# TensorE issues heads 0 to 2's scores one step earlier, ahead of two transposes, with waits per head

## The reference

```
bias = (adj + adj)[:, None]
a = q @ k.T * D**-0.5 + bias            # 16 heads of 32 columns, 512 x 512 each
a = where(any(a != 0, -1), a, -inf)
p = softmax(a); p = where(isnan(p), 0, p)
o = p @ v                               # heads put side by side
x = layernorm(x + o @ Wo.T)
```

## Time and profile before

| what | value |
|---|---|
| time, median of 3 runs | 2225.41 us (2225.25 to 2225.51) |
| the profiled execution's own time | 2224.26 us |
| its span | 2222.5 us |
| granted TensorE clock, mean | 0.989 |
| TensorE busy | 2125.2 us, 96% |
| VectorE busy | 1580.2 us, 71% |
| ScalarE busy | 1570.8 us, 71% |
| GpSimd busy | 301.8 us, 14% |
| chain that ended last, TensorE's share | 71% |

### The profile page before, as it was taken

One profiled execution on the slowest core, in us unless ns is written; L12 is line 12 of the kernel. 1 busy time (PEld: TensorE's weight loads), 2 busy tenths in 40 slices (PEclk: granted clock), 3 DMA queues, 4 the chain that ended last, 5 costly groups with the idle time before them and its releaser, 6 DMA issues.

```text
span 2222.5 us, 42446 instructions
## 1 busy us (share of the span) xinstructions
PE 2125.2 (96%) x14627; PEld 1683.8 (76%) x14627; DVE 1580.2 (71%) x4012; ACT 1570.8 (71%) x3509; POOL 301.8 (14%) x659
## 2 busy tenths in 40 slices
PE   6999999589999999999999999999999999999996
PEld 5778887467777777777777777777777777777774
DVE  5887877366767676767676768686868686868675
ACT  3544443187878787878787878787878787878785
POOL 0000000110202020202020202020202020202011
PEclk9999999799999999999999999999999999999999
DMA  6444342677777777777777777777778777777761
GB/s 237 160 155 148 133 150 94 130 119 127 141 129 139 128 140 128 140 126 142 134 133 133 134 133 135 132 136 132 134 130 138 134 135 131 136 135 133 131 100 45
DMA packets 149008, 297.18 MB, mean 134 GB/s; under 512 B 14514, under 2 KB 14546, under 8 KB 148690
## 3 DMA queue, kind: packets, MB, share of 16 engines
q1 hardware_dynamic: 137490, 256.97, 61.8%
q0 software_dynamic: 11328, 37.76, 6.0%
HBM read 110.12 MB, written 50.33 MB: 72 GB/s over the span
## 4 chain that ended last, share of the span: by engine, by line
PE 71%; issue 13%; ACT 8%; DVE 6%; DMA 1%; POOL 0%; SPq 0%; DVEq 0%; ACTq 0%; POOLq 0%
PE bank L605 28%; PE bank L651 17%; PE bank L635 11%; PE bank L620 8%; ACT prob L872 3%; DVE prob L1166 2%; PE bank L525 2%; ACT probT L770 2%; PE bank L542 2%; PE bank L577 1%; PE bank L643 1%; DVE z L1130 1%; DVE st_ln L1123 1%; DMA qp<-stage_q 1%; ACT v L844 1%
## 5 line engine op out<-in xcount | busy, mean ns | idle before, releaser
L1166 DVE CUSTOM_DVE_ANT_0 prob<-bank,adj_sb 128x512 f32<-128x512 f32 x1024 | 657.7, 686 | 140.8 <-PE bank L620 140.8
L872 ACT ACTIVATE prob<-prob,neg_max 128x512 f32<-128x512 f32 x1024 | 731.3, 723 | 9.4 <-DVE neg_max L1175 5.4
L770 ACT ACTIVATE probT<-bank 128x512 f32<-128x512 f32 x832 | 460.3, 594 | 320.4 <-PE bank L651 318.0
L651 PEld LDWEIGHTS bank<-ident,prob 128*128 128x128 f32 x4096 | 463.6, 140 | 111.9 <-issue 51.9
L651 PE MATMUL bank<-ident,prob 128*128 128x128 f32 x4096 | 541.1, 275 | 5.6 <-ACT probT L770 4.3
L620 PE MATMUL bank<-kp,qp 128*128 128x512 f32 x1024 | 348.5, 422 | 31.1 <-DVE row_max L1166 21.6
L1180 DVE COPY probT<-bank 128x512 f32<-128x512 f32 x192 | 131.6, 686 | 235.9 <-PE bank L651 235.9
L635 PE MATMUL bank<-probT,v 128*32 128x256 f32 x4096 | 247.6, 382 | 0.8 <-issue 0.8
L620 PEld LDWEIGHTS bank<-kp,qp 128*128 128x128 f32 x1024 | 176.4, 190 | 64.5 <-DVE row_max L1166 34.4
L872 ACT ACTIVATION_READ_ACCUMULATOR prob<-prob,neg_max 128x1 f32 x1024 | 204.4, 200 | 0.0
L605 PE MATMUL bank<-xT,wkT 128*128 128x512 f32 x768 | 202.3, 399 | 0.0
(11 more groups left out here) (112 smaller groups left out, 2088.7 us busy)
## 6 DMA issues: line engine op xcount, KB each, us to landing
kp<-stage_k SPq DMA_DIRECT2D x256, 256.0 KB, 6.7
qp<-stage_q SPq DMA_DIRECT2D x256, 256.0 KB, 8.5
x_raw<-in_x_dram SPq DMA_DIRECT2D x16, 1024.0 KB, 7.5
adj_raw<-in_adj_t_dram SPq DMA_DIRECT2D x16, 1024.0 KB, 9.7
outT_spill<-outT SPq DMA_DIRECT2D x16, 1024.0 KB, 5.1
v<-outT_spill SPq DMA_DIRECT2D x16, 1024.0 KB, 15.1
z<-in_x_dram POOLq DMA_DIRECT2D x64, 256.0 KB, 3.1
adj_sb<-in_adj_dram SPq DMA_DIRECT2D x64, 256.0 KB, 8.1
```

Source lines behind the costliest of these rows:

```text
L651: ins = nc.tensor.transpose(t_bank[j % 2][:, mt * P:(mt + 1) * P], prob[:, s % 2, j, mt * P:(mt + 1) * P], ident[:, :])
L770: return nc.scalar.activation(dst, src, ACT.Copy, scale=scale)
L872: nc.scalar.activation(prob[:, s % 2, j, :], prob[:, s % 2, j, :], ACT.Exp, scale=2.0, bias=neg_max[:, s % 2, j:j + 1], accum_out=row_sum[ ...
L1166: nc.vector.tensor_tensor_reduce(prob[:, s % 2, j, :], s_bank[j][:, :], adj_sb[:, t, :], 1.0, LOWEST, ALU.add, ALU.max, row_max[:, g % 2, ...
```

## The change

In the diff, `scores` is called with step s+2 for heads 0 to 2, after the second dense half and ahead of the transposes of heads 2 and 3; it is called with step s+1 for head 3 as before. The prologue issues one such set more. The scores of heads 0 to 2 now wait each for its own bank: head 0 for all four maxima of the step before the one that it belongs to (bank 0 was last read by head 3), head 1 for the second and head 2 for the third maximum. On VectorE each head waits for the transposes of the same head of the step two before.

```diff
-                if heads[0] == 0:
-                    need(pe, s_max, 64 * b + J * s)
-                else:
-                    pe.wait_ge(s_max, 64 * b + J * s + 1)
                 for j in heads:
+                    if j == 3:
+                        pe.wait_ge(s_max, 64 * b + J * s + 1)
+                    else:
+                        need(pe, s_max, 64 * b + (J * s if j == 0 else J * (s - 1) + j + 1))
                     mm(s_bank[j][:, :], qp[:, g % 2, j, t * P:(t + 1) * P], kp[:, g % 2, j, :],
                        start=True, stop=True).then_inc(s_ps, 1)
...
             scores(0, 0, (3,))
+            scores(0, 1, (0, 1, 2))
...
-                    def next_scores(heads):
-                        if s + 1 < STEPS:
-                            scores(b, s + 1, heads)
+                    def next_scores(heads, ahead):
+                        if s + ahead < STEPS:
+                            scores(b, s + ahead, heads)
                         elif not last:
-                            scores(b + 1, 0, heads)
+                            scores(b + 1, s + ahead - STEPS, heads)
...
-                    next_scores((0, 1, 2))
...
-                    next_scores((3,))
+                    next_scores((3,), 1)
...
+                    next_scores((0, 1, 2), 2)
                     pe.wait_ge(pT_act, copies_act(b, s, 1))
                     prob_transpose(b, s, 2)
...
                 if heads[0] == 0:
                     dve.wait_ge(adj1_in[t], 16 * b + 16)
-                    need(dve, p_ps, 64 * b + J * (s - 1))
                     if t == 0:
                         need(dve, live_chain, 3 * (G * b + g - 1))
                 for j in heads:
+                    need(dve, p_ps, 64 * b + J * (s - 2) + j + 1)
                     wait_apart(dve, s_ps, 64 * b + J * s + j + 1)
```

## The result

The changed kernel takes 2270.78 us (median of 5 runs, 2268.62 to 2272.95) against 2225.51 us; the ratio is 1.0205, 95% interval [1.0192, 1.0218]. The profiled execution took 2268.62 us with a span of 2266.8 us, 44.3 us over the span before. The granted clock is 1.00 in the batches of both kernels, so it has no part in this. The forecast was 2259 us in a range of 2240 to 2277. A batch lasts 113.57 us from its last transposes to the next batch's, mean of 14, against 110.86.

The account below looks back on a forecast made before the run. TensorE, busy 109.35 of 110.8 us a batch, was taken as the bound. Terms 1.56 + 0 + 0.60 + 0.25 - 0.65 + 0.13 = 1.89 a batch, x14 = 26.5, with the ends 33.9 us: 2259.3, range 2240 to 2277.

Parts of the forecast that it names:

- Part 1: Steps 1, 3, 11, 13, 14, 15: head 3's score waits 0.16 us, loses 0.10 overlap; 1.56 per batch.
- E+1.39: Start of head 3's score, 1.39 us after the recorded end of the transposes closing a step; 1.90 before the change.
- Part 2: Heads 0 to 2's scores, made two steps ahead, wait for head 3's maximum: 0.16 us to spare, cost 0.
- Part 3: Transposes of heads 2 and 3 come 0.70 us later; through ScalarE's ReLU, Y in step 5 comes 0.60 later.
- Part 4: Step 4's spread of reciprocals: its chain comes 0.45 us later with 0.2 spare; cost 0.25.
- Part 5: Gains: step 8's wait at head 3's score shrinks 0.30 us, step 9's transpose waits filled, 0.35; sum -0.65.
- Part 6: Step 14: next batch's head 0 scores wait for the fourth packed-q transfer; +0.13 us, bounds 0 and 0.7.
- The ends: Outside the middle batches: batch 0 costs about 3.4 us, the last batch 4.0.
- Rival (c): Slower: head 3's maximum late in odd steps or q's last pair 0.7 later; 0.7 to 1.0 a batch, 2272; chance 0.2.
- (a): Faster: early scores keep VectorE fed, step 8's wait at head 3's score goes whole; 2202 us, chance 0.06.
- (b): No change: needs bias-to-score hand-over of 0.58, not 0.74; gains and Y's delay cancel; 2226 us, chance 0.06.
- S3(9): Head 3's score for step 9, issued in step 8: still late by about 0.9 us, waiting for VectorE.

Follow-up runs that it names:

- the first run: Changed kernel, per-head waits kept, with heads 0 to 2's scores back in their old place; 2225.0 us, ratio 1.0002.
- the run with step 6 alone: Kernel before, with the per-head waits and only step 8's scores made early, in step 6; 2220.78 us, ratio 0.9983.
- the run with three waits taken away: Kernel before with per-head waits, step 8's scores early, its bias ahead of copy, ReLUs one step earlier, step 9's heads 0 and 1 copied before x; 2221.28 us.

## Why the prediction was right, and where not

- Part 1, S3 behind the copy: right to 0.04, place and price. Steps 1, 3, 11 and 13 grew by 0.27 to 0.30 for 0.26. Step 15 grew by 0.22 because it also lost the 0.08 that it used to wait for q. E+1.39 came as written. It is shown by the bias ahead of the copy.
- Part 2, no wait at S012 for head 3's maximum: right; the odd steps show S3's 0.27 and little else (0.03 or 0.04 in steps 3, 11 and 15 is not explained). No price of the per-head waits: shown by the first run, in the old place.
- Part 3, Y in step 5: 0.59 for 0.60, shown by step 4 in the old place.
- Part 4, the spread in step 4: 0.23 for 0.25. It went with the bias ahead of the copy.
- Part 5, step 8: -0.40 for -0.30, the mechanism (ScalarE's copy limits it) seen in the run with step 6 alone. Step 9 failed: -0.02 for -0.35. I let S012(11) fill the wait at T2, and forgot that S012(10) had left the same stretch: T2 waits for a copy that hangs on step 8's last dense matmul, from which it stands 3.46 us away in both kernels. The matmuls between are as many as before. In step 9 of batch 5 of the changed kernel, with step 8's last dense matmul at 1073.94:

```profile
1074.38 0.60 ACT L771 ACTIVATE v<-bank 128x512 f32<-128x512 f32 x1 [1.39 <-PE bank L605]
...
1076.76 1.07 ACT L771 ACTIVATE probT<-bank 128x512 f32<-128x512 f32 x2
...
1077.40 0.90 PEld L651 LDWEIGHTS bank<-ident,prob 128*128 128x128 f32 x8 [0.82 <-ACT probT L771]
```

ScalarE waits for the dense work, copies v, and then goes on without a gap, through two exponentials and the copy of x, to the copy that T2 waits for. From its copy of v to T2 it is 3.03 in each of batches 1 to 14 of both kernels. The wait at T2 did not fill, it grew: from 0.32 on the weight load to 0.82. No run moves step 9's scores alone. But the run with three waits taken away bears out that ScalarE's order sets this wait: with heads 0 and 1 copied ahead of x, step 9 fell by 0.28.

- Part 6, q: the mechanism was right and the size wrong: 0.13 forecast, 0.54 measured (0.89 in step 14 less S3's 0.27, and less the 0.08 that step 15 no longer waits). I wrote that the last pair "queue behind the first pair, which I take to hide it". It does, but the queue itself had moved, from k's packing on: q landed 0.41 later, which is the whole of what was missing. The bound of 0.7 held it. The 2 us of fixed cost in the Trainium skill (DMA: Bandwidth & Descriptors, Latency and other measured facts) is no guide under such a queue: the last transfer of the next batch's q took 7.2 to 9.8 us from issue to landing in all of these kernels (batches 2 to 13).
- The ends: up to the end of batch 0 it cost 3.5 for 3.4, the last batch 2.9 for 4.0. The first agreement is in part luck: 0.7 of the 3.5 comes before step 1 of batch 0, and the end of batch 0 lies at 551.2 us in the kernel before and at 552.8 in the one with the old place and the new waits, for no reason that the change gives.
- Together: (2.71 - 1.89) x 14 = 11.5 us more, 1.1 less at the end, which is the 10 us between forecast and span. Rival (c) had q's delay as one of its two ways, at 0.7 to 1.0 a batch; it came at half of that. Rivals (a) and (b) are out: no step but 8 gained clearly, and the hand-over from bias to S3 stayed at 0.74, where (b) needed 0.58.
- Of the signs, TensorE's wait in more places, Y and S3(9) (0.89 late by its weight load) came as written, and so did VectorE's wait ahead of its copy. One did not: VectorE's idle time before scores was to nearly vanish, and 95.0 of 140.8 us are left.
- The range held, but with the two misses on the same side: step 9 and q together are 0.74 a batch, 10 us.

The Trainium skill (PSUM — Partial Sum Buffer, Engine vs sequencer instructions) says that matmuls start in program order, while a weight load may overlap matmuls in flight. The trace agrees: S3 of step 8 starts at 1066.20, and the 32 matmuls of weigh_v behind it start 0.43 later, though the last copy that they read had ended at 1065.54.

## What to carry to other kernels

On an in-order engine, moving work earlier makes something else later by just as much: list who waits for the pieces that were overtaken, follow each chain until it comes back to the engine, and compare with the slack it has there. Here the early scores cost six times 0.27 us because the overtaken transposes led, through a copy and a bias, to the next score. Idle time of the engine that is not the bound (140.8 us here) is no gain in store, and a transfer that lands just in time will turn any wait that is removed ahead of it into a wait for itself: count its queue from its first neighbour, not from its own issue. Before moving much, try the order on the waiting engine: one instruction swapped on VectorE undid 27 us of this change.

## What the runs showed of the hardware

- A 512-column matmul that has to wait costs 0.10 to 0.12 us beyond the wait (0.35 to the next block's start for 0.23), and such a wait can leave no trace on the matmul row: in the changed kernel 90 waits, of 0.16 us in step 15, show no idle time there, and 0.43 us on the weight load's row.
- From the start of a 128x512 bias with maximum on VectorE to the start of the matmul that waits for it: 0.74 to 0.76 us in all traces.
- Transfers of 256 KB between SBUF tiles, the four of the next batch's q in a row on SyncE's queue, land 1.2 to 2.2 us apart on average, and the last lands 13.5 to 14.4 us after the last dense matmul of step 12. Its own issue does not decide that: in the run with the bias ahead of the copy it was issued 0.6 us sooner than in the changed kernel (5.13 and 5.74) and landed 0.2 later.
